# Row sums in column tiles, last rows loaded in pairs, and a new order of the work between two layers

## The reference, cut to what matters

```python
x = x + _L0_conv_ref(_gn(x), w_real, w_imag, b_real, b_imag)
x = x + _L1_conv_ref(_gn(x))
```

## Time and profile before

| what | us |
|---|---|
| median of 3 runs | 4363.12 |
| lowest, highest | 4359.79, 4365.41 |
| the profiled execution | 4364.15 |
| its span in the trace | 4362.3 |
| PE busy | 3915.1 (90%) |
| DVE busy | 3150.0 (72%) |
| ACT busy | 2601.1 (60%) |
| POOL busy | 2618.4 (60%) |
| row sums, PE L462, 1024 records | 531.1 busy |

### The profile page before, as it was taken

The page is one execution under the profiler, slowest core; times in us unless marked ns, Lnnn a source line. Parts: engine busy times, 40 slices in busy tenths (PEclk is TensorE's granted clock), DMA queues, the critical chain, the costliest instruction groups (busy, mean ns, idle before and its releaser), DMA issues.

```text
span 4362.3 us, 120693 instructions
## 1 busy us (share of the span) xinstructions
PE 3915.1 (90%) x40080; PEld 2612.7 (60%) x40080; DVE 3150.0 (72%) x5901; ACT 2601.1 (60%) x4768; POOL 2618.4 (60%) x2177
## 2 busy tenths in 40 slices
PE   4299898998989989899898998989988998989988
PEld 1166664666646666466655666556665665656667
DVE  7778775787757877578766886668866787757876
ACT  0189722996239952499425993179822797229962
POOL 4088651886428854388535884268842787418865
PEclk9699998999989999899998999989999999989999
DMA  7311174112731137211371114711156111651114
GB/s 162 135 49 51 41 207 106 51 51 60 208 88 51 51 87 198 70 49 52 109 205 40 51 48 125 188 41 53 42 155 167 41 53 34 188 133 51 51 45 136
DMA packets 221876, 405.99 MB, mean 93 GB/s; under 512 B 96048, under 2 KB 171168, under 8 KB 205216
## 3 DMA queue, kind: packets, MB, share of 16 engines
q1 hardware_dynamic: 221600, 402.52, 33.9%
HBM read 255.55 MB, written 146.80 MB: 92 GB/s over the span
## 4 chain that ended last, share of the span: by engine, by line
PE 72%; POOL 9%; DVE 8%; issue 5%; DMA 3%; ACT 2%; SPq 1%; POOLq 0%; DVEq 0%; ACTq 0%
PE p L535 20%; PE h_ps L609 13%; PE h_ps L428 13%; PE p L462 9%; PE p L635 5%; PE xt_ps L418 4%; POOL ob_all L1172 3%; POOL arena L1165 2%; DMA img<-in_x 2%; PE p L579 2%; PE h_ps L535 2%; POOL ob_all L1174 2%; POOL arena L1188 1%; PE p L435 1%; DVE ob_all L898 1%
## 5 line engine op out<-in xcount | busy, mean ns | idle before, releaser
L535 PE MATMUL p<-arena,bd_all 64*64 64x512 f16 x16896 | 1230.7, 380 | 17.9 <-DVE ob_all L1042 9.2
L1165 POOL TENSOR_TENSOR arena<-arena 128x512 f16<-128x512 f32 x512 | 593.1, 1158 | 646.5 <-ACT arena L700 567.0
L680 ACT ACTIVATE arena<-h_ps 128x512 f16<-128x512 f32 x512 | 305.7, 597 | 959.6 <-PE h_ps L609 729.5
L535 PEld LDWEIGHTS p<-arena,bd_all 64*64 64x64 f16 x16896 | 617.5, 105 | 388.7 <-issue 191.6
L1223 POOL TENSOR_TENSOR arena<-img 128x512 f32<-128x512 f32 x392 | 497.8, 1271 | 581.0 <-PE h_ps L609 553.0
L428 PE MATMUL h_ps<-hilbert,arena 128*128 128x256 f16 (+1 forms) x6240 | 794.7, 278 | 30.5 <-DVE arena L1009 25.9
L428 PEld LDWEIGHTS h_ps<-hilbert,arena 128*128 128x128 f16 (+1 forms) x6240 | 616.3, 99 | 175.0 <-issue 36.1
L1174 POOL TENSOR_TENSOR ob_all<-ob_all,img 128x512 f32<-128x512 f32 x512 | 663.1, 1295 | 82.9 <-POOL ob_all L1172 72.9
L1172 POOL TENSOR_TENSOR ob_all<-ob_all 128x512 f32<-128x512 f32 x512 | 654.5, 1278 | 21.2 <-DVE ob_all L1042 21.2
L1009 DVE SCALAR_TENSOR_TENSOR arena<-h_ps,arena 128x512 f16<-128x512 f32 x512 | 354.1, 692 | 390.0 <-ACT arena L714 389.1
L462 PE MATMUL p<-img,bd_all 128*48 128x512 f32 x1024 | 531.1, 628 | 115.8 <-DMA img<-in_x 77.9
(11 more groups left out here) (154 smaller groups left out, 4462.4 us busy)
## 6 DMA issues: line engine op xcount, KB each, us to landing
img<-in_x SPq DMA_DIRECT2D x256, 512.0 KB, 6.9
out<-ob_all SPq DMA_DIRECT2D x512, 256.0 KB, 3.1
bd_all<-bd_dram SPq DMA_DIRECT2D x512, 192.0 KB, 2.2
wrap_mat<-tab_wrap_h SPq DMA_DIRECT2D x512, 32.0 KB, 2.0
bd_dram<-ob_all SPq DMA_DIRECT2D x16, 768.0 KB, 3.5
arena<-tab_hilbert_kernel SPq DMA_DIRECT2D x8, 256.0 KB, 3.4
hilbert<-tab_hilbert SPq DMA_DIRECT2D x1, 522.0 KB, 3.5
cosw<-tab_cosw SPq DMA_DIRECT2D x1, 320.0 KB, 3.0
```

The lines of the kernel that those rows point to most:

```text
L535: m = mm(bank[out_half * HP:(out_half + 1) * HP, :], low(half, 6 * lm + (j if own else j + 1)), (g_part if own else h_part)(half, lp), sta ...
L1165: G.tensor_tensor(gp[s][:, 1, :], g32, gp[s][:, 0, :], ALU.subtract).then_inc(g_split, 1)
```

## The change

Four things, all outside the rows of layer 0.

1. Row sums. The weights of a row get 16 columns of zeros, so that they are 64 wide. A pair of rows is summed together: the even row into partitions 0 to 63 of `uv_ps`, the odd row into 64 to 127. A pair is cut into two parts of 256 columns, and layer 1 runs one part per step, from u = 17 on (`sum_part`). The virtual rows are then 128 partitions high (`NV`), of which the upper 64 are the odd rows' share; `vmat`, `to_virtual`, `from_virtual` and `stack_virtual` hold their entries twice. The two halves meet in the products with `stack_virtual` and `from_virtual`.
2. Loads. Rows 48 to 63 of the next image come in pairs, in two DMAs of 256 KB each: at j = 28, 29, 30 and 31 the pairs 2j-8 and 2j. PE and VectorE wait for each pair by itself.
3. Order in layer 0. The product with `to_virtual` goes to the end of the layer before. The `c_tab` products and what VectorE makes of them go behind the products of the virtual rows. `stack_virtual` and `from_virtual` go in front of the Hilbert product of row 1.
4. `vbase` is made by ACT and no longer by VectorE.

```diff
+            def load_pair(b, t):
+                for i in range(2):
+                    sp.dma_start(img[i * HP:(i + 1) * HP, t:t + 2, :].rearrange("p t w -> p (t w)"),
+                                 x_v[b, i, :, :, t * W:(t + 2) * W]).then_inc(loaded_pair[(t - (T - LAG)) // 2], 16)
...
-                    if j >= 5 and j % 2 == 1 and k <= NCH - 3:
+                    if j >= 5 and j % 2 == 1 and k < NCH - LAG // CHUNK:
                         refill(b, k)
-                    if j == T // 2 - 3:
-                        refill(b, NCH - 2)
-                refill(b, NCH - 1)
+                    if 2 * j >= T - R - 1:
+                        load_pair(b + 1, 2 * j - R - 1)
+                        load_pair(b + 1, 2 * j)
...
+            def virtual_scales(b):
+                pe.wait_ge(s_scale, b * 2 + 1)
+                mm(c_ps[0:NV, 18:20], tb["to_virtual"][:], sc[:, 8:10], start=True, stop=True).then_inc(s_vsum, 1)
...
-            def sum_row(b, k, s, r, row, start=False, stop=False):
-
-                if r == 0:
-                    pe.wait_ge(loaded[s], b * 32 + 32)
-                    pe.wait_ge(uvw_ready, b * NCH + k + 1)
-                w = uvw[s % 2][:, 3 * r:3 * r + 3, :].rearrange("p j c -> p (j c)")
-                m = mm(uv_ps[0:NV, :], w, img[:, row, :], start=start, stop=stop)
-                if r == CHUNK - 1:
+            def sum_part(b, q, part):
+
+                k, r = q * 2 // CHUNK, q * 2 % CHUNK
+                if part == 0:
+                    wait_rows(pe, b, 2 * q)
+                    if r == 0:
+                        pe.wait_ge(uvw_ready, b * NCH + k + 1)
+                cols = slice(part * HALF, (part + 1) * HALF)
+                for i in range(2):
+                    w = uvw[k % 2][:, 4 * (r + i):4 * (r + i) + 4, :].rearrange("p j c -> p (j c)")
+                    m = mm(uv_ps[i * HP:(i + 1) * HP, cols], w, img[:, 2 * q + i, cols],
+                           start=(q == 0 and part == 0), stop=(q == T // 2 - 1 and part == 1),
+                           skip_group_check=True)
+                if r == CHUNK - 2 and part == 1:
                     m.then_inc(uv_summed, 1)
...
             def layer0(b):
-                pe.wait_ge(s_scale, b * 2 + 1)
-                mm(c_ps[0:NV, 18:20], tb["to_virtual"][:], sc[:, 8:10], start=True, stop=True).then_inc(s_vsum, 1)
-                pe.wait_ge(kappa_made, b + 1)
-                for i in range(3):
-                    for f in range(3):
-                        m = mm(c_tab[:, i], block_mat[:, 3 * i + f, :], kappa[:, f], start=(f == 0), stop=(f == 2))
-                m.then_inc(c_made, 1)
...
                 m.then_inc(v_mixed, 1)
+                pe.wait_ge(kappa_made, b + 1)
+                for i in range(3):
+                    for f in range(3):
+                        m = mm(c_tab[:, i], block_mat[:, 3 * i + f, :], kappa[:, f], start=(f == 0), stop=(f == 2))
+                m.then_inc(c_made, 1)
                 front_hilbert(b * T)
                 front_turn(b * T + 1, 1)
+                pe.wait_ge(v_rows, b + 1)
+                mm(p0[2], tb["stack_virtual"][:], vrow[0:NV, :, :], start=True, stop=True).then_inc(v_stacked, 1)
+                pe.wait_ge(v_means, b + 1)
...
-                    if follow and u >= LAG:
-                        row = u - LAG
-                        sum_row(b + 1, row // CHUNK, row // CHUNK, row % CHUNK, row, start=(row == 0))
+                    if follow and u > LAG:
+                        sum_part(b + 1, (u - LAG - 1) // 2, (u - LAG - 1) % 2)
                 if follow:
+                    sum_part(b + 1, (T - LAG) // 2 - 1, 1)
...
                     group_variance(b * 2 + 3)
+                    virtual_scales(b + 1)
...
+                def virtual_base():
+
+                    act.wait_ge(v_mixed, b + 1)
+                    act.wait_ge(edge_kept, b + 1)
+                    for a in range(2):
+                        ins = nc.scalar.activation(vbase[0:NV, a, :], p0[0][0:NV, a * HALF:(a + 1) * HALF], ACT.Identity,
+                                                   bias=edge[0:NV, 6 + a:7 + a], scale=unscale[0:NV])
+                    ins.then_inc(vbase_made, 1)
```

More of the change, by code:

```diff
@@ L63 @@
 USES = [len(range(s, T // 2, NS)) for s in range(NS)]
-NV = 3 * C
+NU = 3 * C
+NV = P
 QUARTER = HALF // 4
@@ L224, in build @@
         vmat_spaced, vmat_in = sem("vmat_spaced"), sem("vmat_in")
-        loaded = [sem(f"loaded{k}") for k in range(NCH)]
+        loaded = [sem(f"loaded{k}") for k in range(NCH - LAG // CHUNK)]
+        loaded_pair = [sem(f"loaded_pair{q}") for q in range(LAG // 2)]
         uvw_ready, uv_summed, rows_counted = sem("uvw_ready"), sem("uv_summed"), sem("rows_counted")
@@ L337, in _ @@
             sp.wait_ge(vmat_spaced, 1)
-            for k in range(3):
-                sp.dma_start(vmat[k * C:(k + 1) * C, :, :].rearrange("p j m -> p (j m)"),
-                             spaced16[32 * k:32 * k + C, :, :].rearrange("p j m -> p (j m)")).then_inc(vmat_in, 16)
-            sp.wait_ge(vmat_in, 48)
+            for at in (0, HP):
+                for k in range(3):
+                    sp.dma_start(vmat[at + k * C:at + (k + 1) * C, :, at:at + NU],
+                                 spaced16[32 * k:32 * k + C, :, :]).then_inc(vmat_in, 16)
+            sp.wait_ge(vmat_in, 96)
             sp.wait_ge(setup_done, 1)
-            for k in range(NCH - SCRATCH // CHUNK, NCH):
-                load(0, k)
+            for t in range(T - LAG, T, 2):
+                load_pair(0, t)
             for g in range(T // GROUP_T):
@@ L367, in refill @@
             def refill(b, k):
-                last = (k + 1) * CHUNK - 1
-                if last < T - K:
-                    sp.wait_ge(moved, b * NDIFF + last + 1)
-                elif last <= T - R - 2:
-                    sp.wait_ge(turned, b * T + last + R + 2)
-                else:
-                    sp.wait_ge(row_out, PRIMED + b * T + last + 1)
+                sp.wait_ge(moved, b * NDIFF + (k + 1) * CHUNK)
                 load(b + 1, k)
@@ L581, in layer0 @@
                 front(0, 0, 0)
-                pe.wait_ge(v_rows, b + 1)
-                mm(p0[2], tb["stack_virtual"][:], vrow[0:NV, :, :], start=True, stop=True).then_inc(v_stacked, 1)
-                pe.wait_ge(v_means, b + 1)
-                for j in range(3):
-                    m = mm(c_ps[:, 40 + 2 * j:42 + 2 * j], tb["from_virtual"][:, j, :], vmean[:], start=True, stop=True)
-                m.then_inc(v_meant, 1)
                 mix(0, 0, 0)
@@ L820, in _ @@
             V.memset(flat[:, 0:4 * 144], 0.0)
+            V.memset(vmat[:], 0.0)
             V.memset(spaced, 0.0).then_inc(zeroed, 1)
@@ L996, in layer0 @@
                 lk(V.tensor_tensor(t1[0:NV], t1[0:NV], t2[0:NV], ALU.add))
-                for a in range(2):
-                    ins = V.tensor_scalar(vbase[0:NV, a, :], p0[0][0:NV, a * HALF:(a + 1) * HALF],
-                                          edge[0:NV, 2 + a:3 + a], unscale[0:NV], ALU.add, ALU.mult)
-                lk(ins)
+                dve.wait_ge(vbase_made, b + 1)
                 V.tensor_tensor(vrow[0:NV], vbase[0:NV], t1[0:NV], ALU.add).then_inc(v_rows, 1)
```

63 lines of the change are left out of this document (38 added, 25 removed).

## The result

| kernel | median us | range | to the kernel before, 95% interval |
|---|---|---|---|
| before, same chip | 4364.26 | 4359.79 to 4366.56 | 1 |
| changed | 4180.98 | 4176.01 to 4193.10 | 0.9585 [0.9572, 0.9598] |

What follows compares the result with a forecast made beforehand. PE was taken to bound the kernel, being all of layer 1's chain with sums. Savings of 49 (loop), 5 (sum at u = 16), 49 (tail) and 20 (order) made 123 us: 4240, own range 4200 to 4275, 8 in 10 4150 to 4320.

Steps and rivals of the forecast that it cites:

- 1, the sums in the loop: Layer 1 steps: a sum part falls from 0.99 to 0.84 us, records partly overlapping; 49 us saved, 5 more at u = 16.
- Rival A: Layer 1 sums: both column halves run wholly beside each other, part 0.56, step 2.15, saving 138; total 4149 us; chance 19%.
- rival C: Layer 1: loads of the next image set the step, which can't get below 2.57 us; total 4290; chance 8%.
- 2, the tail: Between images: fewer bytes loaded after the last output row, `group_mean` about 16 us after it instead of 23; 49 us saved.
- 3, the order: Layer 0 before row 1: 3.4 us gained before the virtual rows' products, 1 lost behind; 20 us over 8 images, bounds 3 to 32.
- my terms 3.9 and 0.5: Before the virtual rows: transposes start 3.9 us earlier without `block_mat` products ahead; 0.5 from `to_virtual` not waiting for PE's jump.
- theory (d): Layer 0 before row 1, formed after the result: order worth twice the forecast, as PE's whole wait behind the virtual rows went.
- 4, the start: Program start: a memset of `vmat` and more, smaller DMAs lie under other work; 0 us, bounds -1 and +4.
- Rivals B: Layer 1 sums: no overlap in float32, loop saves 0 or loses 33 us; total 4304 to 4337; chance 12%.
- D: Layer 1 sums: weight loads come into the open, part 1.47, step 3.05 us; slower than before, total 4476; chance 6%.
- E: Layer 1: step bound by a wait mistaken for PE work; only tail and order gains count, 4290 to 4300 us; chance 5%.

## Why the prediction came out 60 us high

**1, the sums in the loop: the size was wrong, and a step of the reasoning.** I took 0.84 for a part because the odd row's first record should be held back behind the even row's second. It isn't: each part of the changed kernel has its records in just this order, and the part is 0.58; with four in a row per tile two streams still run at once. In the changed kernel the four records start two by two, as the records of line L480 in two stretches of 0.1 and 0.15 us show (count, shortest, median and longest in ns):

```profile
L480 PE MATMUL p<-img,bd_all x2: 430/430/430, 1084.6 to 1084.6; 128*64 128x256 f32 x2
...
L480 PE MATMUL p<-img,bd_all x4: 379/404/430, 1084.6 to 1084.9; 128*64 128x256 f32 x4
```

I had looked for starts at 0, 0.22, 0.27, 0.49; two are there by 1084.70 and four by 1085.00. Rival A, to which I gave 19%, had the mechanism and the size: part 0.56, step 2.15, against 0.58 and steps of 2.15 and 2.26 in turn. The Trainium skill (TensorE: Matmul & The Clock Gate, Part 3: Packing small matmuls — row/col tiling) pointed the same way, and here the runs agree: 1.01 in one tile, 0.58 in two, the shape change included in both.

**Its rest was given back.** Rival A expected 138 from the steps; rows 16 to 63 gave 98. With the loads in front of the stores in both kernels it is 126.13 - 109.50 = 16.63, and 16.63 x 7 = 116. What is missing from there to 138 is mostly the second step of each two, 2.26 where A had 2.15. So 18 us of the loop's gain went to late loads, which is the mechanism of rival C in part. The other 15 of the 33 that the earlier loads are worth lie in rows 0 to 16, and these loads were late in the kernel before as well. I had set C aside because the rate of the loads would stay below one seen elsewhere. The rate was not the limit: the loads are late by the time they stand behind a store in SP's queue, and by 6.3 us of landing. The row with which I argued, 10.3 us from issue to use, was the right one, but I compared it with landing times alone and left out the queue in front.

**2, the tail: right in sum.** Counts and the last sums start 8.3 after the last output where I took 6.5: I counted 1.5 MB behind it, but from 1180 to 1189 the DMA engines were full and moved 281 GB/s, 2.5 MB, so some 1 MB issued earlier was still under way (an estimate from that row). `group_mean` comes after 16.3 (16) all the same, since my terms had come to 15.1 and were rounded up without a reason, and the 0.65 of waiting in front of the aggregate is gone (1189.06 + 6.03 to 1195.13). The tail gave 46 us against 49; that it came so near is partly luck. That DVE would end last, with PE just in front of it, held too, and so did the point that bytes were what the last loads waited for: with 1 MB more behind the last output, the counts go on at 11.2. I had put all 49 down to the loads; without the paired loads 19 of the 46 are still there (23.75 - 20.99 = 2.76, x 7), by the faster sums.

**3, the order: the sum near by luck, both of its terms wrong.** Undone, the order costs 25 to 28 us, and my 20 with its bounds of 3 to 32 holds that. But in front of the virtual rows' products I took a gain of 3.4 and it is 0.44, and behind them I took a loss of 1 and it is a gain of 4.00 - 1.34 = 2.7, which is beyond my bound of 0.6. In front, the transposes start 3.3 us earlier than before (`group_mean` to the first: 7.50 for 10.78; my terms 3.9 and 0.5 made it 4.4). Then 1.9 go up to the first product of the virtual rows, since PE idles there (3.23 in front of the first transpose, 1.12 behind it) and the stretch up to 1212 has a granted clock of 0.66, that is partly 1.2 GHz, which I had not counted. Behind the virtual rows the wait of 3.02 fell to 0.67, and the products that moved there run at 2.4 GHz.

The table has 39 and not 25, because the products with `vmat` all run at 2.4 GHz even with the order undone. That is the 14 for which my sum had no term. My theory (d), that the whole 39 is the order's, fell with it.

**4, the start:** nothing to be seen, as taken.

**The range.** 4181 lies outside the forecast's own range of 4200 to 4275. It lies inside 4150 to 4320 because that range was drawn out to rival A, and A was right on the column tiles. One reading was off without effect: the earlier trace rows has 2.47 for the 36 products of the mix, and I divided 2.40.

Rivals B, D and E fell: float32 overlaps across column tiles, weight loads never came into the open, and the step was PE's. D rested on a sentence of the Trainium skill (TensorE: Matmul & The Clock Gate, Part 3), by which a weight load overlaps a running product only in another row group. (The same part also allows loads ahead into a background weight buffer.) All sums share one row group, their loads take 0.13 us, and each tile still has a record every 0.216: the measurement decides against the sentence as it stands.

## What to carry to other kernels

Where a product uses half of the array's columns, try a second one beside it in the other column half. Here it was nearly free, in float32 as well, and needed no special order. When a step then gets shorter, look at what was issued a fixed number of steps ahead: count the time of its queue, waits of the stores in front included, against the new step, not its bandwidth. And judge an edge stage not only by when its first work can start but by whether PE stays busy: here the new order let the transposes start 3.2 us earlier, and 2.8 of that was gone by the last virtual product, because PE idled in between and ran partly at 1.2 GHz. Last, undo each part of a change before its share is read from two traces: 39 us stood in the stretches of the order, and 25 were its own.

## What the runs showed of the hardware that was not expected

Program order on PE does not serialise column tiles: with four records in a row for one tile and four for the other, both tiles ran at full pace, 0.216 us a record, in float32. That is the pace of one tile alone in the run with both rows in one tile.

A small DVE operation took up to 0.93 us for 0.34 beside an operation of POOL. Line by line, before and after (shortest, median, longest in ns):

```profile
L964 DVE TENSOR_SCALAR kappa<-stat,sc x8: 340/396/927, 193.9 to 3897.3; 128x128 f32<-128x128 f32 x8
```

```profile
L995 DVE TENSOR_SCALAR kappa<-stat,sc x8: 343/343/347, 194.6 to 3715.2; 128x128 f32<-128x128 f32 x8
```

The 927 ns one started at 1249.62, while POOL's 1.15 us `TENSOR_TENSOR` had run since 1249.30. Of the eight before, the four that overlapped with POOL's operation by more than 0.3 us took 449 to 927 ns, the other four 340 to 343. In the changed kernel no POOL operation falls there. That POOL slows it was only read from the overlap, not tested.
